# Attention and expert kernel: PSUM cut into single banks, smaller jobs between the score pairs, value products two steps behind

## What is computed

```python
q, k, v = (x @ W.T + b for q, k, v)          # reshaped to (B, L, H, Dh)
q, k = _rope(q, sin, cos), _rope(k, sin, cos)
scores = jnp.einsum('bqhd,bkhd->bhqk', q, k) / jnp.sqrt(jnp.float32(Dh))
attn = jax.nn.softmax(scores, axis=-1)
out = jnp.einsum('bhqk,bkhd->bqhd', attn, v).reshape(B, L, D) @ Wo.T + bo
x1 = _layernorm(x + out)
out0 = _moe_group(x1, router_w0, wg0, wu0, wd0, TOP_K)   # and out1 with the second set
x = _layernorm(x1 + (out0 * TOP_K + out1 * TOP_K) / (TOP_K + TOP_K))
```

## Time and profile before

| | |
|---|---|
| runs | 3250.47, 3251.36, 3258.52 us; median 3251.36 |
| profiled execution | 3237.55 us, span 3235.7 us |
| granted TensorE clock, mean | 0.850 |
| PE busy | 2509.7 us (78%) |
| DVE busy | 1992.6 us (62%) |
| ACT busy | 1426.1 us (44%) |
| POOL busy | 1153.5 us (36%) |

### The profile page before, as it was taken

One profiled execution on the slowest core, in us unless ns is written; L12 is line 12 of the kernel. 1 busy time (PEld: TensorE's weight loads), 2 busy tenths in 40 slices (PEclk: granted clock), 3 DMA queues, 4 the chain that ended last, 5 costly groups with the idle time before them and its releaser, 6 DMA issues. The chain is left out here.

```text
span 3235.7 us, 42420 instructions
## 1 busy us (share of the span) xinstructions
PE 2509.7 (78%) x12271; PEld 1252.0 (39%) x12271; DVE 1992.6 (62%) x3695; ACT 1426.1 (44%) x2982; POOL 1153.5 (36%) x936
## 2 busy tenths in 40 slices
PE   3899999799789789889889889527676777777750
PEld 1433434334334334334334333215555555555540
DVE  3687787688688788778778772354222233444458
ACT  0277666566556556556557565101121122222213
POOL 1222122322322222232232210245555545666664
PEclk6699999889989989989989996657788888888775
DMA  4224432423333324324324220158555556554456
GB/s 129 68 78 101 117 97 77 86 83 91 78 79 92 87 64 106 81 68 111 80 56 111 78 52 24 30 158 295 154 152 154 157 144 199 154 168 132 127 175 228
DMA packets 226414, 365.75 MB, mean 113 GB/s; under 512 B 56400, under 2 KB 163792, under 8 KB 221968
## 3 DMA queue, kind: packets, MB, share of 16 engines
q1 hardware_dynamic: 186224, 279.18, 31.5%
q0 software_dynamic: 31648, 75.48, 7.6%
q10 hardware_dynamic: 8320, 8.39, 0.8%
HBM read 204.60 MB, written 132.09 MB: 104 GB/s over the span
## 5 line engine op out<-in xcount | busy, mean ns | idle before, releaser
L848 DVE TENSOR_REDUCE maxima_sb<-ps_a 128x1 f32<-128x1024 f32 x1024 | 1203.2, 1217 | 297.2 <-PE ps_a L597 263.4
L476 ACT ACTIVATE probs_sb<-ps_b 128x512 f32<-128x512 f32 x2048 | 1070.5, 601 | 482.4 <-PE ps_b L587 406.4
L597 PE MATMUL ps_a<-k_stack_sb,q_stack_sb 48*128 48x512 f32 x2048 | 721.6, 463 | 176.0 <-DVE maxima_sb L848 98.0
L587 PE MATMUL ps_b<-q_stack_sb,k_stack_sb 50*128 50x512 f32 x2048 | 834.9, 489 | 18.7 <-issue 10.7
L597 PEld LDWEIGHTS ps_a<-k_stack_sb,q_stack_sb 48*128 48x128 f32 x2048 | 336.6, 198 | 687.9 <-DVE maxima_sb L848 511.6
L616 PE MATMUL ps_o<-probs_sb,v_sb_sb 128*32 128x512 f32 x4096 | 591.9, 652 | 0.0
L1246 PE MATMUL ps_g<-w_gu_sb,x_cols_sb 128*128 x1272 | 417.3, 459 | 95.1 <-ACT x_cols_sb L1199 48.4
L587 PEld LDWEIGHTS ps_b<-q_stack_sb,k_stack_sb 50*128 50x128 f32 x2048 | 350.4, 197 | 214.2 <-ACT probs_sb L476 134.0
L1372 DVE TENSOR_TENSOR hidden_sb<-gate_sb,ps_g 128x128 f32<-128x128 f32 x318 | 91.2, 287 | 494.9 <-ACT gate_sb L1206 272.2
L1199 ACT ACTIVATE x_cols_sb<-ps_x 128x256 f32<-128x256 f32 x318 | 122.1, 384 | 466.4 <-PE ps_x L1235 261.7
L1246 PEld LDWEIGHTS ps_g<-w_gu_sb,x_cols_sb 128*128 128x128 f32 x1272 | 261.6, 228 | 155.2 <-issue 124.3
(11 more groups left out here) (136 smaller groups left out, 2318.7 us busy)
## 6 DMA issues: line engine op xcount, KB each, us to landing
x_rows_sb<-rows_dram SPq DMA_DIRECT2D x159, 129.0 KB
y_dram<-y_rows_sb SPq DMA_DIRECT2D x159, 128.0 KB
rows_dram<-blank_sb SPq DMA_DIRECT2D x39, 516.0 KB, 5.1
swapped_sb<-feat_qk_sb SPq DMA_DIRECT2D x64, 256.0 KB, 3.7
parts_dram<-parts_q_sb SPq DMA_DIRECT2D x16, 1024.0 KB, 4.0
parts_dram<-parts_k_sb SPq DMA_DIRECT2D x16, 1024.0 KB, 4.0
q_stack_sb<-parts_dram SPq DMA_DIRECT2D x64, 256.0 KB
k_stack_sb<-parts_dram SPq DMA_DIRECT2D x64, 256.0 KB
```

Of the source, the lines that this page charges most:

```text
L476: act.activation(probs[t % 2][:, j, :], src[:, :], ACT.Exp, scale=float(DH) ** -0.5).then_inc(s_bdrain, 1)
L587: pe.matmul(out[:, :], k_stack[u % NSTK][lo:lo + XROWS, jj, kc * P:(kc + 1) * P].bitcast(F32R), q_stack[u % NSTK][lo:lo + XROWS, jj, qh * ...
L597: ins = pe.matmul(out[:, kh, :], q_stack[u % NSTK][lo:lo + ROWS, jj, qt * P:(qt + 1) * P].bitcast(F32R), k_stack[u % NSTK][lo:lo + ROWS, j ...
L848: vec.tensor_reduce(maxima[u % 2][:, 1 - k, i:i + 1], src[:, :, :].rearrange("p a q -> p (a q)"), AX.X, ALU.max).then_inc(s_adrain, 1)
```

## The change

It changes these things, all in the attention phase:

- `ps_a` is three single banks instead of two double ones, `ps_b` four banks instead of three. PSUM's eight banks are all in use, as before.
- Each plain score matmul has a bank and a reduction of its own (512 wide), four a step. The two halves' maxima are joined by one more DVE instruction per unit (`row_max`).
- Q and K come in quarters of 256 tokens, V in blocks of 128, O in blocks of 128: twice to four times as many jobs, each of two matmuls 256 wide. R is two jobs, S and R.
- A step has two halves, `k` = 0 and 1, with two score pairs each. Jobs have a half: M, T, L and S stand in the first, behind the value product, the rest in the second. `between` is called in each half with room 2, so a piece of cost 6 goes into each.
- O is due at steps 10 to 17 instead of 14 and 16.
- The value product of step t-2 stands between the two halves of step t (before: that of t-1 behind the four pairs). There are three `probs`. ACT's copy of `ps_o` stands behind the step's four exponentials.
- V lies as 17 columns a head, 16 values and a 1; a matmul still loads 32 columns.
- SP moves a whole unit's output in five transfers (four heads and the sums) instead of two for each half.

```diff
-NBR, NAR = 3, 2
+NBR, NAR, NPR = 4, 3, 3
+VW = DH + 1
+PV_LAG = 2
...
-        for c, at in enumerate((start - 46, start - 20)):
-            for half in range(2):
-                put(b_jobs, at + 2 * half, "Q", b, c, half)
-                put(b_jobs, at + 4 + 2 * half, "K", b, c, half)
+        for c, at in enumerate((start - 46, start - 20)):
+            for q in range(QUARTERS):
+                put(b_jobs, at + q, 1, "Q", b, c, q)
+                put(b_jobs, at + QUARTERS + q, 1, "K", b, c, q)
+        for i in range(KC):
+            put(b_jobs, start - 7 + i, 1, "V", b, i)
+            put(a_jobs, end + 10 + i, 1, "O", b, i)
         for i in range(KC // 2):
-            put(b_jobs, start - 8 + 2 * i, "V", b, i)
-            put(b_jobs, end + 37 + i, "T", b, i)
-        for i in range(KC // 4):
-            put(a_jobs, end + 14 + 2 * i, "O", b, i)
+            put(b_jobs, end + 37 + i, 0, "T", b, i)
...
-        ps_a = [ps(f"ps_a{i}", [P, 2, HALF]) for i in range(NAR)]
+        ps_a = [ps(f"ps_a{i}", [P, HALF]) for i in range(NAR)]
...
-            def o_out(n):
+            def o_out(u):
...
+                sp.wait_ge(s_ocp, 2 * (u + 1))
...
+                for j in range(G):
+                    lo = (g % 2) * G * DH + j * DH
+                    sp.dma_start(o_feat[b % 2][lo:lo + DH, g // 2, :].rearrange("p (a l) -> p a l", a=2),
+                                 o_raw[32 * j:32 * j + DH, :, :]).then_inc(s_oraw, 16)
+                sp.dma_start(dram["den"][b, g * G:(g + 1) * G, :].rearrange("h (a l) -> h a l", a=2),
+                             o_raw[DH:P:32, :, :]).then_inc(s_oraw, 16)
...
                 for k in range(2):
-                    out = a_tile() if in_a else None
                     for kh in range(2):
-                        if in_a:
-                            score(ta, 1 - k, kh, out)
-                        if in_b:
+                        if 0 <= ta < n_steps:
+                            score(ta, 1 - k, kh)
+                        if 0 <= t < n_steps:
                             score_t(t, HEADS[2 * k + kh])
-                if 1 <= t <= n_steps:
-                    pv(t - 1)
+                    if k == 0 and 0 <= t - PV_LAG < n_steps:
+                        pv(t - PV_LAG)
...
-                room = 4 if 0 <= t + LEAD < n_steps else 1 << 30
+                room = 2 if 0 <= t + LEAD < n_steps else 1 << 30
...
-                    for k in range(2):
-                        src = arrived()
-                        vec.tensor_reduce(maxima[u % 2][:, 1 - k, i:i + 1], src[:, :, :].rearrange("p a q -> p (a q)"), AX.X,
-                                          ALU.max).then_inc(s_adrain, 1)
-                between(t)
+                for k in range(2):
+                    for kh in range(2):
+                        if 0 <= ta < n_steps:
+                            src = arrived()
+                            vec.tensor_reduce(maxima[u % 2][:, 1 - k, i, kh:kh + 1], src[:, :], AX.X,
+                                              ALU.max).then_inc(s_adrain, 1)
+                    between(t)
```

More of the change, by code:

```diff
@@ L54, in schedule @@
     b_jobs, a_jobs = {}, {}
-    put = lambda jobs, t, *job: jobs.setdefault(t, []).append(job)
+    put = lambda jobs, t, k, *job: jobs.setdefault((t, k), []).append(job)
     for b in range(nb):
@@ L167, in attention_phase @@
         s_den = sem("den_moved")
-        s_oraw = [sem(f"o_raw_out{i}") for i in range(2)]
+        s_oraw = sem("o_raw_out")
         s_swap, s_parts = sem("swapped_in"), sem("parts_out")
@@ L437, in arrived, with features @@
                 return ps_b[(filled[0] - 1) % NBR]
-            def features(which, b, c, half):
+            def features(which, b, c, q):
                 src = arrived()
@@ L446, in features @@
                         act.wait_ge(s_afill, a_no[("L", b - 2)] + 1)
-                act.activation(feat[which][:, half * HALF:(half + 1) * HALF], src[:, :], ACT.Identity,
+                act.activation(feat[which][:, q * QUARTER:(q + 1) * QUARTER], src[:, 0:QUARTER], ACT.Identity,
                                bias=bias[:, which, c:c + 1]).then_inc(s_bdrain, 1)
@@ L493, in _ @@
+                if 0 <= n < n_steps and n % KC == KC - 1:
+                    done = n // KC
+                    act.wait_ge(s_pv, n + 1)
+                    if done >= 2 and done % 2 == 0:
+                        act.wait_ge(s_oraw, 16 * (G + 1) * (done // 2))
+                    act.activation(o_raw[:, done % 2, :], ps_o[:, :], ACT.Copy).then_inc(s_ocp, 1)
                 for b in range(nb):
@@ L523, in features @@
                 for dc in range(DC):
-                    ins = pe.matmul(out[:, :], w[:, dc, c * P:(c + 1) * P], x_t[:, dc, half * HALF:(half + 1) * HALF],
+                    ins = pe.matmul(out[:, 0:QUARTER], w[:, dc, c * P:(c + 1) * P], x_t[:, dc, q * QUARTER:(q + 1) * QUARTER],
                                     start=dc == 0, stop=dc == DC - 1)
@@ L529, in values @@
                 out = b_tile()
-                for a in range(2):
-                    tok = (2 * i + a) * P
-                    for dc in range(DC):
-                        ins = pe.matmul(out[:, a * D:(a + 1) * D], x_t[:, dc, tok:tok + P], w_v[:, dc, :],
-                                        start=dc == 0, stop=dc == DC - 1)
+                for dc in range(DC):
+                    ins = pe.matmul(out[:, 0:D], x_t[:, dc, i * P:(i + 1) * P], w_v[:, dc, :],
+                                    start=dc == 0, stop=dc == DC - 1)
                 ins.then_inc(s_bfill, 1)
@@ L554, in project_out @@
                 pe.wait_ge(s_pool, norm_o_done(b))
-                for a in range(4):
-                    tok = (4 * i + a) * P
-                    for c in range(DC):
-                        ins = pe.matmul(out[:, a // 2, a % 2 * D:(a % 2 + 1) * D], o_feat[b % 2][:, c, tok:tok + P], w_o[:, c, :],
-                                        start=c == 0, stop=c == DC - 1)
+                for c in range(DC):
+                    ins = pe.matmul(out[:, 0:D], o_feat[b % 2][:, c, i * P:(i + 1) * P], w_o[:, c, :],
+                                    start=c == 0, stop=c == DC - 1)
                 ins.then_inc(s_afill, 1)
@@ L589, in score_t, with score @@
                           start=True, stop=True).then_inc(s_bfill, 1)
-            def score(ta, side, kh, out):
+            def score(ta, side, kh):
                 u, i = divmod(ta, STEPS)
+                out = a_tile()
                 if i == 0 and kh == 0 and side == 1:
```

248 lines of the change are left out of this document (121 added, 127 removed).

## The result

The changed kernel takes 3269.6 us (median of 20 runs, 3251.1 to 3285.5), the kernel before beside it 3248.2 (20 runs): the ratio is 1.0068, 95% interval 1.0047 to 1.0088. It is slower by 0.7%, where the prediction had it 39 us faster. The profiled execution took 3271.8 us; that of before, 3237.6, was a short one of its kind.

The account below looks back on a forecast made before the run. No engine is full; a loop through freed score banks bounds a step at 2.62 us. About 8 us for each of five batches (40), +3 first, -5 second, +3 last, -2 lead-in: 39 us off, 3212 us, range 3115 to 3279.

Parts of the forecast that it names:

- I count 3 us for a short overlap and 1 for low clock: Steps 0 to 17: 3 us lost where POOL's list meets SP's stacks, 1 us to a lower PE clock.
- The rival: POOL's list alone delays PE's completions beside the projections: about 14 of its 20 us lost, six batches, 3278 us; chance 0.14.
- the 5.1 us of gain: Steps 0 to 17 of a middle batch, with the projection: 70.2 us where before it was 75.3.
- nearly all of it PE: Last batch's 21 steps without reductions: 4.08 us each at half clock, mostly PE's work; the change adds 0.1 each.
- job step: Attention step holding a job: score pairs, value product and a job of 1.06 make 3.39 us.
- free step: Step with nothing else in it: a loop over three banks and four reductions takes 2.58 us, against 2.62 before.
- V, steps 56 to 63: End of a batch: seven job steps and a free one take 26.3 us instead of 28.9, counted as 1.8 gained.
- a `ps_o` copy in a free step: Every eighth step the next value product waits 0.5 us for ACT's copy; four counted, 2 us lost a batch.
- the new maximum: DVE's extra instruction joining two halves: 0.2 to 2.3 us, mean 0.5, four times a batch; 1 us lost.
- The whole fixed cost: Rival on DVE: each 512-wide reduction takes 0.66 us without overlap, giving 3254 us, no change; chance 0.1.
- The reciprocal did not stay late: Refers to a rival before the projection: late input or POOL holds the reciprocal, 8.7 us in six batches, 3264; chance 0.06.
- More comes off: Rival on attention steps: job steps fall to 3.1 us and free steps to 2.4, giving 3122 us; chance 0.2.

Follow-up runs that it names:

- new_paced: Changed kernel with POOL's 16 list transfers of a batch spread one per step instead of one every 1.27 us; 3198.8 us, ratio 0.985 to the kernel before.
- old_paced: Kernel before the change with its POOL list transfers spread one per step in the same way; 3204.3 us, ratio 0.986 to the unedited kernel before.
- old_profiled: Kernel before the change, unedited, run for a profile in the third job, on a chip of 3236 us; its steps 14 to 17 take 35.6 us.

## Why the prediction was wrong

**The step that failed** is "*I count 3 us for a short overlap and 1 for low clock*" in the projection. I took the stacks for the cause of the late completions, since they began 1 us after the stacks were issued and had not begun with the list alone. But the on-time exponentials at 1126.44 stood only 8.4 us behind the start of the list (1118.05), and in the six batches of that trace the first late one was due 9.2 to 10.2 us behind it. Over steps 0 to 17 of the third to eighth batch the changed kernel took 91 us more than new_paced, where I had 18. The rival was named, with a chance of 0.14, and the list as the cause was right: it priced 14 us lost in each list, and 15 were. Its course was another, on time for 7 us, then two late ones, then nothing for ten, instead of 1.41 us for each completion. Its total of 3278 lies near the measured 3269.6 by luck in part, since the end of the last batch gave some 37 us that it did not have. What I held against the rival was one row, from a moment at which it would have looked the same.

**The gain was not there either.** The 75.3 us of steps 0 to 17 before, from which the 5.1 us of gain were counted, contain the late completions of the kernel before. With the list spread in both, these steps take 67.0 us before (old_paced) and 70.4 with the change, and the third to seventh batch together 1212.7 and 1212.9. So without late completions the change does not shorten the middle batches; what it gains is at the end of the last one, 22 us between these two profiles.

**The second error went the other way.** I gave the last 21 steps +0.1 us each, "*nearly all of it PE*" at half clock. They run at full clock after the change: the last 19 take 36.6 us less instead of 2 more. PE is busy 94% of the time at either level (74.15 of 79.09 us at 0.50, 40.19 of 42.48 at 1.00), so PE sets the pace, and its clock what that is. The gain varies: in before, old_profiled and old_paced these steps take 79.1, 70.1 and 65.7 us, the clock falling sooner or later, and 42.5 to 43.7 in every profile with both the lag and the bank. I had not asked whether a change of the order could keep the clock up. It does with the two together; why one alone is not enough is not shown.

**The profiled execution** came out 73 us above the 3198.5 forecast for it: late completions +73 (91 less 18), last batch's end -39, expert phase +25 (969 us in the profile before, 994 after, 962 to 992 in the others of these chips, in no order: scatter, not the change), and 14 for the rest.

**Point by point**, in us, of the fifth batch where nothing else is said:

| | forecast | measured |
|---|---|---|
| job step | 3.39 | 3.38 |
| free step | 2.58 | 2.70 |
| steps 0 to 9 | 30.1 | 31.67 |
| reciprocal, after the batch's start | 17.6 | 18.6 (1099.99) |
| wait before the first projection | 8.4 | 8.26 |
| steps 0 to 17 | 70.2 | 70.4 in new_paced, 85.3 in the changed kernel |
| second batch, steps 0 to 17, lost | 8 | 9.0 |
| second batch, whole, lost | 5 | 7.5 |
| each Q and K stage | 27.1 | 28.4 and 27.68 |
| steps 37 to 43 (T and L) | 0.3 gained | 2.7 lost, 1.2 to 1.5 in the other middle batches |
| V, steps 56 to 63 | 1.8 gained | 0.6 lost (35.3 instead of 34.7) |
| a `ps_o` copy in a free step | 0.5 | 0.48 (3.18 instead of 2.70) |
| the new maximum, mean | 0.5 | 1.06 (33.9 for 32), up to 4.08 |

The loop of the free step was right and its pieces a little short: from the reduction's start to the freed pair 0.74 (0.71 taken), to the value product 0.43 (0.33), then 1.00 and 0.53. That is 1.7 us a batch. The new maximum went above its upper bound of 2.3. In V, step 57 takes 8.75 us, with DVE's small instructions beside POOL's rotation (its first instruction runs from 1303.67 to 1306.02):

```profile
1303.72 2.33 DVE L755 CAST expert_sb<-top_idx_sb 128x16 f32<-128x16 uint32 x1
1305.97 1.27 DVE L853 TENSOR_REDUCE maxima_sb<-ps_a 128x1 f32<-128x512 f32 x2
1307.17 1.20 DVE L755 CAST expert_sb<-top_idx_sb 128x16 f32<-128x16 uint32 x1
```

**The other rivals.** The whole fixed cost falls: four reductions take 2.48 us (1106.20 to 1108.68), which is three pitches of 0.60 and one of 0.68, not 4 x 0.66. The reciprocal did not stay late. More comes off: no, job steps stayed at 3.38.

## What to carry to other kernels

An operation that looks harmless in its first microseconds may only need longer to bite: before a row is taken as evidence that a transfer holds up nothing, look at how long it had been going, and at its end. Spread GpSimd's transfers over the steps when PE's completions are wanted meanwhile, as the runs on two of three chips bear out; it costs one wait each. Before a gain is counted from the measured time of a stage, ask what of that time has a cause that the change leaves in place. When a change leaves PE less idle, ask whether its clock stays up, and price the stage at both levels; and where PE waits for a chain with a known length, move the consumer behind it before making the steps shorter.

## What the runs showed of the hardware

On two of three chips PE's completions come late at ACT and DVE when POOL issues indirect transfers every 1.27 us. The first late exponential was due 4.5 to 10.2 us behind the first transfer, in every list or burst of eight that lay beside the scores. In the changed kernel two come late while the list goes out (by 2.6 and 1.5 us in the fifth batch), and the next only when it is out, 10 us on; in the kernel before they come late one at a time, by 0.8 to 3.4 us. One transfer a step (3.4 us) does nothing of the kind. On the third chip lists in one piece show none of it, and the expert phase takes 782 to 786 us instead of 962 to 994 with the same instructions, at much the same time for one of POOL's transfers (0.96 us both). Every run on record comes with a granted clock, so it was traced; whether completions are late in an untraced run is not shown.

Steps without reductions took 4.16 us at the clock of 0.50 (79.09 for 19) and, in another order, 2.24 at 1.00 (42.48 for 19).
